# Transposed masks kept in DRAM: a graph-attention kernel on one Trainium2 core

## The chip, the cores and the metric

The kernel runs on one core of a Trainium2 chip. Time is device time in microseconds (us), median of several runs. The engines are TensorE (PE, matrix products; its weight loads are listed as PEld), VectorE (DVE), ScalarE (ACT), GpSimd (POOL) and SyncE (SP), which here does nothing but wait and issue DMAs. Each engine works off its own instructions in order.

## The reference, cut to what matters

```
x = layernorm(x + L0(x, adj))          # one attention stage over a 1024-node graph, 8 graphs, 256 features
mask = adj + eye > 0
for l in range(3):                     # the graph layers
    s_i, s_j = x @ attn_w[l, :256], x @ attn_w[l, 256:]
    scores = leaky_relu(s_i[:, None] + s_j[None, :] + attn_b[l], 0.2)
    attn = softmax(where(mask, scores, -inf))
    h = layernorm(x + attn @ x)
    x = layernorm(h + gelu(h @ W1[l] + b1[l]) @ W2[l] + b2[l])
out = layernorm(x_in + x)
```

`x` is (8, 1024, 256), `adj` (8, 1024, 1024), `W1` (3, 256, 1024). The mask is the same in all three layers.

## The kernel before, in words

A first stage (0 to about 575 us) computes `L0` and writes two things to DRAM: the rows `x` and an additive mask `mask`, bf16, 0 where there is an edge and -1e30 where not, by rows. Then come the graph layers. The unit is a chunk of 512 rows of one graph (BANK = 512); there are C = 16 chunks in a layer and K = 48 over three layers. In the loop over k every engine works on several chunks at once: TensorE transposes chunk k - 1's normalised rows (L1553), aggregates chunk k (L1575 to L1577), then runs chunk k - 1's feed-forward part, `up` (L43 to L45) and `down` (L1626 to L1628), over eight blocks f. One pass of that loop is called a step in what follows, "step k", counted from the transposes on L1553 at its head. Products are made of three passes over high and low parts; the low part is made by VectorE (`pT_lo` L1302, `g_lo` L1391, `h_lo` L1386), the high one by ScalarE.

The softmax numerator is needed with the neighbour j on the partitions, so the mask is needed transposed: `maskT`, [128, 8, 512] bf16, in two halves of four blocks. SP loads each half by a transposing DMA (`load_maskT`, L858), two chunks ahead. VectorE makes the unmasked scores `t` (L1295); GpSimd issues an accumulating DMA that adds `maskT` to `t` in SBUF, in four groups g (`add_masks`, L1100, semaphores `s_tm[g]`); ScalarE then takes the exponential twice (L1169, L1170). The untransposed mask is loaded too (`load_mask`, L851), a row block at a time into a ring of three, for the row maxima (`row_top`, L1281).

All of SP's DMAs stand in one order written out by hand. Per step it issues: `load_x` (even k, L843), `load_r` (odd k, L879), `load_raw` (L882, L884; raw weights of the next layer, steps 4 to 11 of a layer but the last), two row masks, at a new layer three pieces of the split weights (`load_split`, L907), the store of chunk k - 2's rows (L935), the first half of `maskT` for chunk k + 2, the store of `rline` (L872), `vline` (L863), `store_split` (L901), two more pieces, `load_v` (L868), `load_r`, two more masks, the second half of `maskT`, the last three pieces, and in the third layer only here the store of the output rows (L932). A wait in front of one of them holds all behind it.

At a layer's start TensorE computes a product of `b2` with all eight pieces of the new `W1` (`fold_b2`, L1604, 32 matmuls with two columns each) between the aggregation and the first `up`; it waits for all pieces. `raw_hi` (L1217) on ScalarE turns a raw piece into its high part, between the GELUs of blocks 1 and 2; `x_hi` (L1160) stands behind block 2. In the third layer ScalarE's `n2` (L1194) writes `xo`, and waits for the store of the chunk before.

Of the kernel before, what the change touches and what calls it, by code (L numbers as in the profile page):

```python
# [12 lines left out]
P = 128  # L13
F32 = mybir.dt.float32
F32R = mybir.dt.float32r
BF16 = mybir.dt.bfloat16
# [8 lines left out]
BANK = 512  # L25
# [602 lines left out]
def layer_buffers(nc, ctx, x, w1, rows, s_rows, uv):  # L628
# [3 lines left out]
    L = Layers()  # L632
# [7 lines left out]
    def sem(name):  # L640
        return ctx.enter_context(nc.semaphore(name))
# [135 lines left out]
    L.s_x_in = s_rows  # L777
    L.s_mask = [sem(f"mask_in{i}") for i in range(MASKS)]
    L.s_maskT = [sem(f"maskT_in{i}") for i in range(2)]
    return L  # L780


def graph_layers(nc, L, x, rows, out, mask, split, vline, rline, par):

    attn_w, attn_b, W1, b1, W2, b2, g1, be1, g2, be2 = par
    B, N, D, F, NT, KD, KF = shapes(x, W1)
# [42 lines left out]
    def tops_of(k):  # L829

        first = TC * k + NT + NT - 1
        return [r for r in range(first, first + TC) if r < NT * NB]

    with nc.Block() as block:
        @block.sync
        def _(sp):
# [16 lines left out]
            def load_maskT(k, half):  # L853
                if k > 0:
                    for g in range(2 * half, 2 * half + 2):
                        sp.wait_ge(L.s_tm[g], 16 * k)
                r = BANK * (k % C)
                sp.dma_start_transpose(L.maskT[:, HALF * half:HALF * (half + 1), :],  # L858
                                       mask_rows[r:r + BANK, BANK * half:BANK * (half + 1)]).then_inc(L.s_maskT[half], 16)

            def store_v(n):
                sp.wait_ge(L.s_vline, n - PB + 1)
# [87 lines left out]
            load_norm2(0)  # L950
            load_attention(1)
            for half in range(2):
                load_maskT(1, half)
            for r in range(NT, NT + NT - 1 + MASKS):
                load_mask(r)

            for k in range(K + 2):
                tops = tops_of(k)
                if k % 2 == 0 and k < K - 2:
                    load_x(k // 2 + 1)  # L960
                if 2 <= k and layer_of(k - 2) == LAYERS - 1:
                    load_x1(k - 2)
                if k % 2 == 1 and k + 2 < K:
                    load_r(k + 2)
                for f in split_at(k):
                    load_raw(layer_of(k) + 1, f)
                for r in tops[:2]:
                    load_mask(r + MASKS)
                arriving = layer_of(k) if k < K and new_layer(k) else 0
                if k == 0:  # L970
                    for f in range(2, KF):
                        first_weights(f)
                if arriving:
                    for f in range(3):
                        load_split(arriving, f)
                if k >= 2 and layer_of(k - 2) < LAYERS - 1:
                    store(k - 2)
                if k + 2 < K:
                    load_maskT(k + 2, 0)
                for n in r_made(k):  # L980
                    store_r(n)
                for n in v_made(k):
                    if n >= PB:
                        store_v(n)
                for f in split_at(k):
                    store_split(layer_of(k) + 1, f)
                if arriving:
                    for f in range(3, KF - 3):
                        load_split(arriving, f)
                for n in v_made(k):  # L990
                    if n >= PB:
                        load_v(n)
                for n in r_made(k):
                    load_r(2 * n)
                for r in tops[2:]:
                    load_mask(r + MASKS)
                if k + 2 < K:
                    load_maskT(k + 2, 1)
                if arriving:
                    for f in range(KF - 3, KF):  # L1000
                        load_split(arriving, f)
                if k >= 2 and layer_of(k - 2) == LAYERS - 1:
                    store(k - 2)
                if 2 <= k <= K and new_layer(k - 1):
                    load_norm2(layer_of(k - 1))
                    if layer_of(k - 1) + 1 < LAYERS:
                        load_attention(layer_of(k - 1) + 1)
# [658 lines left out]
def program(nc, x, adj, L0_W, L0_b, L0_attn, attn_w, attn_b, W1, b1, W2, b2, g1, beta1, g2, beta2, out):  # L1666
# [4 lines left out]
    layers = W1.shape[0]  # L1671
    rows = nc.dram_tensor("rows", (layers * C * TC, P, D), F32, kind="Internal").ap()
    mask = nc.dram_tensor("mask", (B * NT, P, N), BF16, kind="Internal").ap()
    split = nc.dram_tensor("split", (layers - 1, W1.shape[2] // P, P, 4, D), F32, kind="Internal").ap()
    vline = nc.dram_tensor("vline", (layers * B, N), F32, kind="Internal").ap()
    rline = nc.dram_tensor("rline", (layers * B, 2, N), F32, kind="Internal").ap()
# [3 lines left out]
    with ExitStack() as ctx:  # L1680
        x_rows = ctx.enter_context(nc.sbuf_tensor("x_rows", [P, 2, NT, D], F32))
        uv = ctx.enter_context(nc.sbuf_tensor("uv", [P, C, 2, TC], F32))
        s_rows = ctx.enter_context(nc.semaphore("x_in"))
        first_stage(nc, x, adj, L0_W, L0_b, L0_attn, attn_w[0], rows, mask, W1, x_rows, s_rows, uv)
        L = layer_buffers(nc, ctx, x, W1, x_rows, s_rows, uv)
        graph_layers(nc, L, x, chunks, out_chunks, mask, split, vline, rline, par)


# [22 lines left out]
```

## Time and profile before

| | |
|---|---|
| median of 3 runs | 2473.93 us (2473.46 to 2476.73) |
| the profiled execution's own time | 2465.25 us |
| its span | 2463.5 us |
| TensorE busy | 2317.7 us (94%) |
| VectorE, ScalarE, GpSimd busy | 2065.3, 1728.8, 1137.1 us |
| mean granted TensorE clock | 0.973 of 2.4 GHz |
| DMA | 399472 packets, 400.13 MB; 220408 packets under 512 B |

The profile is of one execution. Busy time says how long an engine had work, not how well it used it. TensorE's granted clock is either full (1.00, 2.4 GHz) or half (0.50, 1.2 GHz); the figure for a stretch is a mean. A DMA's time to landing counts from its issue to the last byte's semaphore.

### The profile page before, as it was taken

Reading aid. Unit: us, or ns where it says so; the run is one execution under the profiler, and the core shown is the slowest. Engines: PE = TensorE matmul, PEld = TensorE weight load, DVE = VectorE, ACT = ScalarE, POOL = GpSimd, SP = SyncE. Lnnn points to the kernel's source line nnn. Section 1 sums busy time; section 2 is a strip of 40 time slices with the busy share of each in tenths; the row PEclk is TensorE's granted clock in tenths of the full one; section 3 lists DMA queues with packets and bytes.
Section 4 is the critical chain, followed back from the end, with each engine's and each line's share of the span. In section 5 each row is a group of like instructions: output and inputs, shape, how many; then the busy total and the mean of one; then the engine's idle time right before and its main releaser. Section 6 shows DMA issues by size and latency. Waiting matters only on the chain.

```text
span 2463.5 us, 45033 instructions
## 1 busy us (share of the span) xinstructions
PE 2317.7 (94%) x16056; PEld 2136.5 (87%) x16056; DVE 2065.3 (84%) x4806; ACT 1728.8 (70%) x2780; POOL 1137.1 (46%) x1317
## 2 busy tenths in 40 slices
PE   7999999993499999999989999999999999999996
PEld 6999999993499999999979989999998888888996
DVE  5888888886678999998869989998997989889875
ACT  3444444442478888888858888888886788787784
POOL 3555555563234344554424434454453546545431
PEclk9999999996699999999989999999999999999998
DMA  4444444444657777775778677767776676685541
GB/s 144 141 141 140 139 145 149 140 129 97 177 145 192 174 189 197 195 178 161 187 174 193 154 189 198 184 180 189 189 174 171 173 198 160 166 206 148 135 112 43
DMA packets 399472, 400.13 MB, mean 162 GB/s; under 512 B 220408, under 2 KB 315152, under 8 KB 399248
## 3 DMA queue, kind: packets, MB, share of 16 engines
q1 hardware_dynamic: 371600, 296.58, 44.4%
q0 software_dynamic: 27648, 100.68, 17.8%
q8 instruction: 127, 2.08, 0.4%
q14 instruction: 97, 0.79, 0.1%
HBM read 187.19 MB, written 58.99 MB: 100 GB/s over the span
## 4 chain that ended last, share of the span: by engine, by line
PE 31%; DVE 18%; DMA 7%; ACT 6%; issue 6%; POOL 4%; SPq 4%; POOLq 0%; ACTq 0%; DVEq 0%
DVE t L1295 5%; PE A L1575 5%; PE A L1576 5%; PE A L1577 5%; DVE g_lo L1391 3%; SPq L858 3%; PE G L45 3%; PE G L43 3%; PE G L44 3%; PE Y L1626 2%; DMA t<-maskT 2%; PE Y L1628 2%; PE Y L1627 2%; DVE spare L1281 2%; DVE st L1321 1%
## 5 line engine op out<-in xcount | busy, mean ns | idle before, releaser
L1575 PE MATMUL A<-x_hi,pT_hi 128*128 128x258 f32 x1536 | 439.3, 286 | 31.5 <-DVE pT_lo L1302 25.2
L1626 PE MATMUL Y<-w,g_hi 128*128 128x256 f32 x1536 | 435.1, 283 | 10.6 <-DVE g_lo L1391 9.8
L1576 PE MATMUL A<-x_hi,pT_lo 128*128 128x258 f32 x1536 | 436.3, 284 | 0.0
L1577 PE MATMUL A<-x_lo,pT_hi 128*128 128x256 f32 x1536 | 433.7, 282 | 0.0
L1627 PE MATMUL Y<-w,g_hi 128*128 128x256 f32 x1536 | 426.8, 278 | 0.0
L1628 PE MATMUL Y<-w,g_lo 128*128 128x256 f32 x1536 | 426.4, 278 | 0.0
L1205 ACT ACTIVATE g<-G,b_less 128x512 f32<-128x512 f32 x384 | 263.6, 686 | 209.6 <-PE G L45 206.7
L1100 POOL DMA_DIRECT2D t<-maskT x192 | 173.8, 969 | 406.9 <-DVE t L1295 402.3
L1302 DVE TENSOR_TENSOR pT_lo<-t,pT_hi 128x512 fp32r<-128x512 f32 x384 | 256.1, 685 | 92.4 <-ACT t L1170 92.2
L1575 PEld LDWEIGHTS A<-x_hi,pT_hi 128*128 128x128 f32 x1536 | 292.5, 190 | 42.4 <-issue 24.2
L1391 DVE TENSOR_TENSOR g_lo<-g,g_hi 128x512 fp32r<-128x512 f32 x384 | 263.8, 687 | 69.4 <-ACT g_hi L1208 69.2
L1626 PEld LDWEIGHTS Y<-w,g_hi 128*128 128x128 f32 x1536 | 288.3, 188 | 33.3 <-DVE g_lo L1391 16.8
L43 PE MATMUL G<-h_hi,w 128*128 128x512 f32 x768 | 308.6, 402 | 5.8 <-DVE h_lo L1386 4.1
L45 PE MATMUL G<-h_lo,w 128*128 128x512 f32 x768 | 305.0, 397 | 0.0
L44 PE MATMUL G<-h_hi,w 128*128 128x512 f32 x768 | 303.6, 395 | 0.0
L1627 PEld LDWEIGHTS Y<-w,g_hi 128*128 128x128 f32 x1536 | 289.6, 189 | 10.6
L1577 PEld LDWEIGHTS A<-x_lo,pT_hi 128*128 128x128 f32 x1536 | 293.0, 191 | 0.0
L1576 PEld LDWEIGHTS A<-x_hi,pT_lo 128*128 128x128 f32 x1536 | 290.9, 189 | 0.0
L1628 PEld LDWEIGHTS Y<-w,g_lo 128*128 128x128 f32 x1536 | 288.7, 188 | 0.0
L1169 ACT ACTIVATE pT_hi<-t,v 128x512 fp32r<-128x512 f32 x384 | 273.1, 711 | 21.7 <-DMA t<-maskT 21.1
L1295 DVE SCALAR_TENSOR_TENSOR t<-rrow,v 128x512 f32<-128x512 f32 x384 | 280.8, 743 | 4.3 <-ACT rrow L1132 4.3
L1170 ACT ACTIVATE t<-t,v 128x512 f32<-128x512 f32 x384 | 272.3, 709 | 0.0
(190 smaller groups left out, 5921.6 us busy)
## 6 DMA issues: line engine op xcount, KB each, us to landing
t<-maskT POOLq DMA_DIRECT2D x192, 512.0 KB, 5.1
mask<-mask SPq DMA_DIRECT2D x192, 256.0 KB, 5.0
a_adj_t<-in_adj SPq DMA_DIRECT2D x64, 512.0 KB, 4.1
x_rows<-rows SPq DMA_DIRECT2D x24, 1024.0 KB, 6.3
rrow<-rline SPq DMA_DIRECT2D x92, 256.0 KB, 4.3
mask<-a_mask SPq DMA_DIRECT2D x64, 256.0 KB, 4.4
rows<-xo SPq DMA_DIRECT2D x32, 512.0 KB, 2.9
vrow<-vline SPq DMA_DIRECT2D x21, 512.0 KB, 4.6
```

Source lines behind the costliest of these rows:

```text
L43: pe.matmul(out, left_hi, right_hi, start=start, stop=False)
L44: pe.matmul(out, left_lo, right_hi, start=False, stop=False)
L45: return pe.matmul(out, left_hi, right_lo, start=False, stop=stop)
L1169: act.activation(L.pT[0][:, n % P_RING, :], L.t[:, j, :], ACT.Exp, bias=bias).then_inc(L.s_exp, 1)
L1295: dve.scalar_tensor_tensor(L.t[:, j, :], L.rrow[:, 0, k % 2, :], L.v8[:, k // 2 % VS, j:j + 1], L.rrow[:, 1, k % 2, :], ALU.add, ALU.max). ...
L1391: dve.tensor_tensor(L.g_lo[:, n % G_RING, :], L.g[:, n % 2, :], L.g_hi[:, n % G_RING, :].bitcast(F32), ALU.subtract).then_inc(L.s_g_lo, 1)
L1575: pe.matmul(L.A[:, t, 0:DE], hi, L.x_hi[:, par, j, :], start=(j == 0), stop=False)
L1576: pe.matmul(L.A[:, t, 0:DE], lo, L.x_hi[:, par, j, :], start=False, stop=False)
L1577: mm = pe.matmul(L.A[:, t, 0:D], hi, L.x_lo[:, par, j, :], start=False, stop=(j == NT - 1))
L1626: pe.matmul(L.Y[:, t, :], hi, w2_part(0, f), start=False, stop=False)
L1627: pe.matmul(L.Y[:, t, :], hi, w2_part(1, f), start=False, stop=False)
L1628: mm = pe.matmul(L.Y[:, t, :], lo, w2_part(0, f), start=False, stop=last and t % 2 == 1)
```

## The change

In the first layer each half of `maskT`, once loaded by the transposing DMA, is also stored as it stands in SBUF to a DRAM tensor `turned`. In the second and third layer `load_maskT` reads that half back with a plain DMA. The stores of chunk k + 1 stand at the head of step k (those of chunk 0 ahead of the loads for chunk 1), each behind a wait for the landing of its half. `load_maskT` waits, besides for `s_tm`, for the store of the chunk before.

```diff
+    L.s_maskT_out = [sem(f"maskT_out{i}") for i in range(2)]
...
                 if k > 0:
                     for g in range(2 * half, 2 * half + 2):
                         sp.wait_ge(L.s_tm[g], 16 * k)
+                    sp.wait_ge(L.s_maskT_out[half], 16 * min(k, C))
+                if k >= C:
+                    sp.dma_start(L.maskT[:, HALF * half:HALF * (half + 1), :], turned[k % C, half]).then_inc(L.s_maskT[half], 16)
+                    return
                 r = BANK * (k % C)
                 sp.dma_start_transpose(L.maskT[:, HALF * half:HALF * (half + 1), :],
                                        mask_rows[r:r + BANK, BANK * half:BANK * (half + 1)]).then_inc(L.s_maskT[half], 16)
+
+            def store_maskT(k, half):
+                sp.wait_ge(L.s_maskT[half], 16 * (k + 1))
+                sp.dma_start(turned[k, half], L.maskT[:, HALF * half:HALF * (half + 1), :]).then_inc(L.s_maskT_out[half], 16)
...
             load_attention(1)
             for half in range(2):
+                store_maskT(0, half)
+            for half in range(2):
                 load_maskT(1, half)
...
             for k in range(K + 2):
                 tops = tops_of(k)
+                if k + 1 < C:
+                    for half in range(2):
+                        store_maskT(k + 1, half)
                 if k % 2 == 0 and k < K - 2:
                     load_x(k // 2 + 1)
...
+    turned = nc.dram_tensor("turned", (C, 2, P, NT // 2, BANK), BF16, kind="Internal").ap()
```

## Rows read from the trace of the kernel before

**Rows 1.** Busy time in steps 9, 14, 17, 20, 21, 32, 33, 35 and 39.
```profile
core 0: us, PE busy (x) PEld busy (x) DVE busy (x) ACT busy (x) POOL busy (x), PEclk, DMA share, GB/s
...
964.60:1000.60 36.00, 35.85 (x259) 33.30 (x258) 32.97 (x77) 30.55 (x50) 16.06 (x16) 1.00 0.68 184
1108.40:1144.10 35.70, 35.70 (x260) 33.34 (x259) 32.38 (x76) 30.27 (x49) 15.46 (x16) 1.00 0.63 163
1251.00:1306.00 55.00, 45.78 (x291) 42.08 (x290) 33.09 (x78) 30.21 (x49) 14.47 (x16) 0.84 0.67 149
1378.10:1414.40 36.30, 35.83 (x259) 33.32 (x258) 32.98 (x77) 31.20 (x52) 18.59 (x26) 1.00 0.79 180
1414.40:1453.10 38.70, 36.77 (x259) 33.70 (x258) 33.21 (x77) 31.48 (x52) 10.28 (x16) 1.00 0.97 205
1812.20:1849.20 37.00, 36.26 (x259) 33.31 (x257) 32.47 (x76) 30.58 (x49) 18.96 (x26) 1.00 0.91 217
1849.20:1898.60 49.40, 44.76 (x291) 41.35 (x291) 32.71 (x78) 29.91 (x49) 15.46 (x16) 0.90 0.63 171
1935.60:1972.70 37.10, 35.91 (x260) 33.36 (x259) 33.45 (x73) 29.07 (x47) 19.97 (x18) 1.00 0.59 156
2084.80:2124.70 39.90, 36.44 (x259) 33.33 (x258) 33.64 (x73) 30.05 (x49) 19.97 (x18) 1.00 0.67 160
```

**Rows 2.** Waits, 690 to 2420 us: us in total, times, longest.
```profile
PE Y L1604 <- DMA w<-split: 12.8, 2, 8.6
...
ACT xo L1194 <- DMA out_rows<-xo: 11.7, 8, 3.7
```

**Rows 3.** SP's queue in step 17: start, duration of the issue, line.
```profile
1247.15 3.52 SPq L858 DMA_TRANSPOSE maskT<-mask  x1
...
1259.71 1.17 SPq L879 DMA_DIRECT2D rrow<-rline  x2
...
1261.92 4.68 SPq L858 DMA_TRANSPOSE maskT<-mask  x1
1266.64 1.53 SPq L907 DMA_DIRECT2D w<-split  x3
```

**Rows 4.** SP's queue in step 33.
```profile
1853.74 4.82 SPq L858 DMA_TRANSPOSE maskT<-mask  x1
1858.60 2.31 SPq L907 DMA_DIRECT2D w<-split  x3
```

**Rows 5.** Busy time behind the first fold, and in a stretch of step 16.
```profile
685.00:692.00 7.00, 7.00 (x24) 6.03 (x24) 3.27 (x9) 1.61 (x2) 0.00 (x0) 0.51 0.44 135
1248.00:1258.00 10.00, 10.00 (x85) 9.78 (x85) 8.13 (x21) 9.02 (x14) 0.16 (x1) 1.00 1.14 124
```

**Rows 6.** TensorE's timeline, the folds of the first and the third layer.
```profile
682.78 4.75 PE L1604 MATMUL Y<-b_parts,w 128*128 128x2 f32 x32
...
1866.22 6.99 PE L1604 MATMUL Y<-b_parts,w 128*128 128x2 f32 x32 [4.24 <-DMA w<-split]
```

**Rows 7.** Timelines and landings of L858 and L884, steps 9, 7 and 20.
```profile
969.04 4.94 SPq L858 DMA_TRANSPOSE maskT<-mask  x1
...
DMA to landing us min/median/max: 6.9/6.9/6.9
...
975.60 0.47 SPq L884 DMA_DIRECT2D x<-in_L_gnn_W  x1
...
DMA to landing us min/median/max: 4.4/4.4/4.4
...
981.24 0.63 ACT L1217 ACTIVATE x<-x 128x512 fp32r<-128x512 f32 x1
...
908.56 0.68 ACT L1208 ACTIVATE g_hi<-G,b_less 128x512 fp32r<-128x512 f32 x1
909.36 0.63 ACT L1217 ACTIVATE x<-x 128x512 fp32r<-128x512 f32 x1
...
1396.69 0.63 ACT L1217 ACTIVATE x<-x 128x512 fp32r<-128x512 f32 x1 [1.77 <-DMA x<-in_L_gnn_W]
```

More of the change, by code:

```diff
@@ L779, in layer_buffers, with graph_layers @@
     L.s_maskT = [sem(f"maskT_in{i}") for i in range(2)]
+    L.s_maskT_out = [sem(f"maskT_out{i}") for i in range(2)]
     return L
-def graph_layers(nc, L, x, rows, out, mask, split, vline, rline, par):
+def graph_layers(nc, L, x, rows, out, mask, turned, split, vline, rline, par):
     attn_w, attn_b, W1, b1, W2, b2, g1, be1, g2, be2 = par
@@ L1685, in program @@
         L = layer_buffers(nc, ctx, x, W1, x_rows, s_rows, uv)
-        graph_layers(nc, L, x, chunks, out_chunks, mask, split, vline, rline, par)
+        graph_layers(nc, L, x, chunks, out_chunks, mask, turned, split, vline, rline, par)
 _INS = ['x', 'adj', 'L0_gnn_W', 'L0_gnn_b', 'L0_gnn_attn', 'L1_gnn_attn_w', 'L1_gnn_attn_b', 'L1_gnn_W1', 'L1_gnn_b1',
```

## The prediction

> **What bounds the kernel now.** I cut the graph layers into steps, one for each pass of the loop over k, from one run of transposes on L1553 to the next, and read TensorE's busy time in each [rows 1]. In step 14 TensorE is busy for all 35.7 us: such a step can't get shorter by anything done to masks. Step 9, in which the weights of the next layer are split as well, takes 36.0 us with TensorE idle for 0.15. So the question is where TensorE idles, and the same view gives the places: step 17 (55.0 us, idle 9.2, mean granted clock 0.84), step 33 (49.4, idle 4.6, clock 0.90), step 21 (38.7), step 32 (37.0), step 39 (39.9), and step 35, one of the plain steps of the third layer, 37.1.
>
> The list of waits says what the idle time waits for [rows 2]. Two waits of the fold of b2 (L1604) for `w<-split` make 12.8 us, the longer 8.6, so the other 4.2: these are steps 17 and 33, where a new layer's weights arrive. ScalarE waits 8 times for the store of the output rows, 11.7 us in all, longest 3.7 (third layer). The third layer's plain steps are longer for another reason as well: step 35 takes 37.1 though ScalarE's waits for the store begin only after it, with VectorE at 33.45 us, more than in steps 9 and 14.
>
> Why are the weights late? The timeline of SP's queue in step 17 [rows 3]: SP is still occupied by the transposing DMA's issue for 3.52 us, and again for 4.68, and only then, at 1266.64, issues the last three pieces of `w`. In step 33 the same: 4.82 us of issue, then the three pieces [rows 4]. All DMAs that matter here stand in this one queue. A plain DMA of as much or more data takes SP about 0.5 us to issue (three in 1.53).
>
> There is a second effect. From 1248 to 1258 the DMA engines are counted as fully busy and move only 124 GB/s [rows 5]. In that stretch the 256-byte pieces of the transpose and the accumulating DMA of POOL (L1100) are under way together; the reload of `rrow` (L879), which waits for the small `rline` store ahead of it, goes out only at 1259.71 [rows 3].
>
> **What the change takes away.** 64 of the 96 transposes (layers two and three) become plain reads of 512 KB, 4 KB to a partition. For each, SP's issue falls from 3.5 to 4.8 us to about 0.5. Worked by places:
>
> Step 17. 3.0 us fall away on the first half's issue and 4.2 on the second's, 7.2 together; and from the end of the first half's issue (1250.67) to the reload at 1259.71 SP stood mostly for the slow stretch, which I take to go with the transposes: some 4 us more at the least, so that the last pieces go out about 11 us earlier than 1266.64. TensorE waited 8.6 us for them [rows 2]. So the wait is gone, not shortened. What is late next is the fold itself. Its price without a wait is seen in the first layer: 4.75 us against 6.99 [rows 6]. It begins there at the full clock (2.4 GHz), yet the clock falls during it, and from 685 to 692 the granted clock is 0.51, 1.2 GHz [rows 5]; of this 4.6 us lie behind the fold, at half speed, a loss of 2.3. A step that holds a fold and no wait is then 36.0 + 4.75 + 2.3 = 43.1 us. Gain in step 17: 55.0 - 43.1 = 11.9.
>
> Step 33. TensorE is free at 1866.22 - 4.24 = 1862.0 and the last piece landed at 1866.2 [rows 6]. Less 4.3 for the issue just ahead of it [rows 4] that is 1861.9, less again what the first half's issue gives: the wait is gone here too. Gain 49.4 - 43.1 = 6.3. If the clock's share were not to come back, the two steps would give 8.6 + 4.2 = 12.8 instead of 18.2.
>
> The Trainium skill ("TensorE: Matmul & The Clock Gate", the part on the HAM clock gate) says that idleness throttles TensorE and activity releases it; taken alone it would let the clock stay high once the wait is gone. The trace does not agree for the fold: rows 5 show 0.51 behind a fold that had no wait before it, though its matmuls of two columns kept the engine occupied. I go by the row; by the page alone the two steps would give some 4 us more.
>
> Step 21 has the same slow stretch and ScalarE's late masks and weights; without it 36.0: gain 2.7. Step 32: 37.0 to 35.7, gain 1.3.
>
> Third layer. SP stores the output rows only behind the second mask half. With both halves short the store goes out some 6 us earlier, the longest wait for it was 3.7, so all eight go. About 0.9 us of each was absorbed: step 39 waited 3.7 and was 39.9 against 37.1, so 2.8 counted. The other seven, 8.0 us together, count 8.0 - 6.3 = 1.7. Gain 4.5, not more, since step 35 shows 37.1 without such a wait.
>
> Sum of gains: 11.9 + 6.3 + 2.7 + 1.3 + 4.5 = 26.7 us.
>
> **What it adds.** 32 stores of 512 KB in the first layer, about 0.5 us of issue each. TensorE doesn't see the 16 us, SP has idle time in each step. The added wait of `load_maskT` for the store is free: the store goes out at the start of a step, the load in its middle or end, and even the transposing DMA of the same size lands within 6.9 us [rows 7]. In layers two and three that wait is for a count reached long before.
>
> What costs is where the stores stand. `store_maskT(k + 1, 1)` waits at the head of a step for a transpose that SP has only just issued. In step 9 the issue ran from 969.04 for 4.94 us and the DMA landed after 6.9, so SP stands for 2.0 us [rows 7], and 0.5 for the second store (the first is issued in the waiting time). Behind it in the queue are `load_x`, `load_r`, `load_raw` and two mask loads; all go out 2.5 us later. Their data then also stand behind 512 KB that were just put on the engines: up to 1.5 us more. Bounds for the delay: 2.0 (wait only) to 5.0 (wait, issue, both stores' data in front); I take 3.0, near the wait plus issue. `load_r` and the masks have many microseconds to spare. `load_raw` (steps 4 to 11) has not: in step 9 its second part landed at 975.60 + 4.4 = 980.0, used at 981.24, 1.2 to spare; in step 7 L1217 starts at 909.36, 0.12 after the GELU before it ended (908.56 + 0.68): ScalarE was waiting already, nothing to spare [rows 7]. ScalarE waits for it in order, with the GELUs behind it, then VectorE's `g_lo`, then TensorE. How much lateness is absorbed shows step 20: ScalarE waited 1.77 us there and the step took 36.3, 0.3 over step 9 [rows 1, 7]; so 1.5 is free. With a delay of 3.0: a step like 7 costs 1.5, a step like 9 costs 0.3. Three steps like 7 and five like 9: 6.0 us. At 2.0 it is 1.5, at 5.0 3 x 3.5 + 5 x 2.3 = 22. `load_x` (every even step) comes ahead of `load_raw` and its use is later in the step; I cost it at nothing beyond that. In the start-up (before step 1) two stores also stand before `load_x(1)`; VectorE needs the result a few us later than it comes: nothing, at most 1.5.
>
> Net: 26.7 - 6.0 = 20.7 us off the profiled execution's 2465.25. That lies 8.7 us under the median of the runs shown; taken as an offset, 2473.93 - 20.7 = 2453.
>
> **The rivals.** A (the forecast, 0.60): as above, 2453. Without any loss in the first layer it would be 2447; should the unprofiled runs owe their 8.7 us more to further slow stretches, 2438.
>
> B (0.22), the gain is half of this: the slow stretch of DMA stays, made by the accumulate with any load beside it. Then the `rline` reload is held up as before, and of 11.9 us in step 17 remain the 4.2 of the second half's issue; steps 21 and 32 give nothing. 4.2 + 6.3 + 4.5 - 6.0 = 9, time 2465. For it: the stretch is the DMA engines' state, and plain reads of the same bytes will be in flight with L1100 too. Against: the packets that crawl are 256 bytes, and there will be none. With the larger first-layer cost (22) B ends at +7; between them lie results within 0.2% (5 us).
>
> C (0.10), slower: the wait at the head of SP's queue. It decides from a delay of about 6.0 us: 3 x 4.5 + 5 x 3.3 = 30 against 26.7. This takes stores that land late enough to hold the loads behind them by 3 us more than I take, in each of the eight steps, with `x_rows` late as well. For it: the engines are loaded there (0.68 of their time in step 9). Time 2477 to 2485.
>
> D (0.08), the change does nothing on the path: the issue time of SP doesn't matter. The Trainium skill ("DMA: Bandwidth & Descriptors", Issuing engines are not separate DMA queues) says the time to initiate a DMA is usually small beside the DMA. By that rule the weights and the output store would land no earlier. Worked out from the rows, steps 17 and 33 and the third layer then stay as they are, and 2.7 + 1.3 - 6.0 is a loss of 2 us: 2476. Rows 3 and 4 speak against it: 4.68 and 4.82 us of issue immediately ahead of the late pieces.
>
> **Numbers.** About 0.2% (5 us) is what this measurement can tell from no change. Faster by more: all of A, most of B, 0.81; within: 0.11; slower: 0.08. Range 2438 (A with the offset regained) to 2468 (B with a somewhat larger loss).
>
> **What would show it.** In the trace after: the two waits L1604 for `w<-split` gone, steps 17 and 33 at about 43 us; SP's plain issue about 0.5; no ScalarE wait for `out_rows`, third-layer steps still 37.1; steps 4 to 11 at 36 to 37.5 with ScalarE idle before L1217. Wrong if those steps grow by over 3 us each, or if `w<-split` still lands last.

## The result and the profile after

The changed kernel takes 2449.74 us (median of 4 runs, 2446.57 to 2455.83); the kernel before took 2474.28 (4 runs, 2473.46 to 2476.73). The ratio is 0.9902, 95% interval 0.9882 to 0.9923: 24.5 us faster, where 20.7 were forecast. A later comparison (kernel 5) gave 2445.72 against 2480.77, ratio 0.9861 (0.9832 to 0.9890). The profiled execution after took 2449.08 us, 16.2 less than the profiled one of before (2465.25). So the profile shows two thirds of the medians' difference; where the rest lies is a question for the experiments.

The steps after, in the same view as [rows 1]: steps 6, 9, 17, 21, 32, 33 and 39.

```profile
core 0: us, PE busy (x) PEld busy (x) DVE busy (x) ACT busy (x) POOL busy (x), PEclk, DMA share, GB/s
...
860.60:898.20 37.60, 36.15 (x260) 33.53 (x259) 33.16 (x77) 31.88 (x53) 13.16 (x26) 1.00 0.93 248
971.30:1007.40 36.10, 35.93 (x260) 33.38 (x259) 32.96 (x77) 29.64 (x48) 11.46 (x16) 1.00 0.79 207
...
1259.10:1302.60 43.50, 41.55 (x291) 38.20 (x290) 32.73 (x78) 30.34 (x49) 15.48 (x16) 0.96 0.60 194
1410.20:1446.20 36.00, 35.87 (x259) 33.34 (x258) 32.95 (x77) 30.37 (x49) 16.07 (x16) 1.00 0.61 178
1805.20:1840.90 35.70, 35.68 (x260) 33.33 (x259) 32.46 (x76) 30.27 (x50) 18.02 (x26) 1.00 0.73 215
1840.90:1887.30 46.40, 44.26 (x291) 40.97 (x290) 32.89 (x78) 30.11 (x49) 15.47 (x16) 0.89 0.57 187
2072.10:2109.20 37.10, 35.90 (x259) 33.35 (x258) 33.62 (x73) 30.15 (x49) 19.99 (x18) 1.00 0.59 172
```

Step 17 went from 55.0 to 43.5 us, step 21 from 38.7 to 36.0, step 32 from 37.0 to 35.7 and step 39 from 39.9 to 37.1. Step 33 came down by 3.0 only, to 46.4, and its granted clock is still 0.89. Step 6 grew from 36.1 to 37.6, as did steps 4, 8 and 11 to between 36.9 and 37.4, while step 9 stayed at 36.1 (36.0 before). The waits that answer to [rows 2], with ScalarE's for the raw weights:

```profile
ACT x L1231 <- DMA x<-in_L_gnn_W: 11.0, 4, 3.1
...
PE Y L1618 <- DMA w<-split: 3.6, 2, 2.1
...
ACT xo L1208 <- DMA out_rows<-xo: 1.1, 2, 0.8
```

The fold waits 3.6 us in all for the split weights, in place of 12.8, and ScalarE 1.1 in place of 11.7 for the output store. New are four waits of ScalarE for the raw weights in the first layer, 11.0 us. SP's queue in step 17 and at the end of its part for step 33, beside [rows 3] and [rows 4]. L860 is the plain read, L916 the split weights, L888 the reload of `rrow`:

```profile
1256.21 0.95 SPq L916 DMA_DIRECT2D w<-split  x2
1259.31 0.85 SPq L888 DMA_DIRECT2D rrow<-rline  x2
...
1261.87 0.33 SPq L860 DMA_DIRECT2D maskT<-turned  x1
1262.24 1.49 SPq L916 DMA_DIRECT2D w<-split  x3
...
1844.71 0.37 SPq L860 DMA_DIRECT2D maskT<-turned  x1
1845.12 1.38 SPq L916 DMA_DIRECT2D w<-split  x3
```

The last three pieces now leave at 1262.24, 3.1 us into the step (before, 15.6 us into it); the reload of `rrow` leaves 3.1 us after the pieces ahead of it, where it took 8.4. The issue of a turned mask half in layers two and three, L860 after:

```profile
L860 SPq DMA_DIRECT2D maskT<-turned x63: 319/327/369, 1188.5 to 2333.0; - x63
...
DMA to landing us min/median/max: 3.4/5.1/7.4
```

and L858 before, over the same layers (ns, minimum/median/maximum, then the landing):

```profile
L858 SPq DMA_TRANSPOSE maskT<-mask x63: 1519/4198/5420, 1184.4 to 2349.6; - x63
...
DMA to landing us min/median/max: 4.0/6.8/12.4
```

So the issue went from a median of 4.2 us to 0.33, and the longest landing from 12.4 us to 7.4. The busy stretch of [rows 5] looks like this after; the last two numbers are the DMA engines' busy share and GB/s:

```profile
1248.00:1258.00 10.00, 10.00 (x71) 9.26 (x70) 10.00 (x27) 7.72 (x13) 5.50 (x5) 1.00 0.95 261
1258.00:1268.00 10.00, 10.00 (x85) 9.80 (x85) 8.11 (x20) 10.00 (x17) 1.52 (x2) 1.00 1.03 348
```

As busy as before, but at 261 and 348 GB/s in place of 124. The first layer shows what was paid. SP's queue in step 6 (L863 transposes, L868 stores, L844 is `load_x`, L891 and L893 are `load_raw`) and ScalarE's reading of the raw weights:

```profile
865.18 5.79 SPq L863 DMA_TRANSPOSE maskT<-mask  x1
871.02 2.37 SPq L868 DMA_DIRECT2D turned<-maskT  x2
873.48 0.38 SPq L844 DMA_DIRECT2D x_rows<-rows  x1
873.91 0.98 SPq L891 DMA_DIRECT2D x<-in_L_gnn_W  x1
874.93 0.69 SPq L893 DMA_DIRECT2D x<-in_L_gnn_W  x1
...
880.48 0.63 ACT L1231 ACTIVATE x<-x 128x512 fp32r<-128x512 f32 x1 [3.09 <-DMA x<-in_L_gnn_W]
```

SP has the first store out at 871.02; the second goes out 2.1 us later, when the transpose lands (7.9 us after its issue), and `load_raw` leaves behind both. Its data land at 880.5, and ScalarE has stood idle for 3.09 us.

### The profile page after: what moved, and what is told of

The parts are those of the page before. It is cut to its first block, busy times and chain, and to the rows that moved or that the text cites. A ratio compares the mean times of both kernels' runs of the same rounds, so it can differ in the third digit from the quotient of the medians.

```text
span 2447.2 us, 45065 instructions
## 1 busy us (share of the span) xinstructions
PE 2316.0 (95%) x16056; PEld 2136.8 (87%) x16056; DVE 2064.6 (84%) x4806; ACT 1729.0 (71%) x2780; POOL 1105.9 (45%) x1317
## 3 DMA queue, kind: packets, MB, share of 16 engines
q0 software_dynamic: 27648, 100.68, 17.1%
## 4 chain that ended last, share of the span: by engine, by line
PE 36%; DVE 19%; DMA 6%; ACT 5%; issue 4%; POOL 4%; SPq 2%; POOLq 0%; ACTq 0%; DVEq 0%
PE A L1589 6%; PE A L1590 6%; PE A L1591 6%; DVE t L1309 6%; DVE g_lo L1405 3%; PE G L45 3%; PE G L43 3%; PE G L44 3%; PE Y L1640 3%; PE Y L1641 3%; PE Y L1642 3%; DVE spare L1295 2%; DMA t<-maskT 1%; DMA x<-in_L_gnn_W 1%; DVE st L1335 1%
## 5 line engine op out<-in xcount | busy, mean ns | idle before, releaser
L1589 PE MATMUL A<-x_hi,pT_hi 128*128 128x258 f32 x1536 | 440.2, 287 | 30.2 <-DVE pT_lo L1316 24.3
```

Source lines behind the costliest of these rows:

```text
L1589: pe.matmul(L.A[:, t, 0:DE], hi, L.x_hi[:, par, j, :], start=(j == 0), stop=False)
```

## The experiments

Each kernel was timed beside the kernel before on the same chip; in the table "before" is its median there. "Spread" is from the lowest to the highest run. The two columns of steps are from the one profiled execution of each: length, the fold's wait for the split weights, and the time at the half clock (1.2 GHz) in that step, added up from stretches of 1 us.

| kernel | median, us | before | ratio (95%) | spread | step 17: us / wait / half clock | step 33 |
|---|---|---|---|---|---|---|
| before, profiled first | | 2474.28 | | 3 | 55.0 / 8.6 / 17.1 | 49.4 / 4.2 / 10.2 |
| changed | 2449.74 | 2474.28 | 0.9902 (0.9882-0.9923) | 9 | 43.6 / 1.4 / 3.4 | 46.4 / 2.1 / 10.2 |
| 1 wait only | 2480.85 | 2477.26 | 1.0015 (0.9998-1.0032) | 17 | 56.4 / 9.8 / 20.5 | 51.2 / 5.7 / 13.7 |
| 2 store only | 2480.68 | 2477.26 | 1.0013 (0.9997-1.0030) | 14 | 52.0 / 6.9 / 13.7 | 49.4 / 4.1 / 13.7 |
| 3 plain, no store | 2448.45 | 2477.26 | 0.9879 (0.9862-0.9896) | 4 | 45.5 / 1.3 / 10.2 | 47.1 / 2.0 / 10.2 |
| 4 order only | 2473.62 | 2477.26 | 0.9981 (0.9966-0.9996) | 17 | 42.0 / 0 / 3.4 | 43.9 / 1.3 / 6.8 |
| 5 changed, again | 2445.72 | 2480.77 | 0.9861 (0.9832-0.9890) | 6 | 41.5 / 0 / 3.4 | 45.9 / 1.3 / 10.2 |
| 6 late store | 2443.57 | 2480.77 | 0.9853 (0.9821-0.9885) | 8 | 46.1 / 1.4 / 10.2 | 43.2 / 1.2 / 3.4 |
| 7 late store and split | 2440.96 | 2480.77 | 0.9837 (0.9808-0.9867) | 9 | 44.1 / 0 / 6.8 | 43.5 / 0 / 6.8 |
| 8 small accumulate | 2440.91 | 2480.77 | 0.9838 (0.9808-0.9867) | 10 | 47.7 / 3.4 / 10.2 | 47.4 / 2.3 / 10.2 |
| 9 plain at two chunks | 2459.71 | 2477.47 | 0.9934 (0.9908-0.9959) | 14 | 42.4 / 0.4 / 3.4 | 42.5 / 0.9 / 3.4 |
| 10 plain elsewhere | 2459.05 | 2477.47 | 0.9931 (0.9904-0.9958) | 20 | 57.9 / 9.8 / 17.1 | 49.0 / 3.8 / 13.7 |
| 11 plain everywhere, late split | 2436.00 | 2477.47 | 0.9838 (0.9808-0.9867) | 8 | 43.9 / 0 / 6.8 | 42.5 / 0 / 3.4 |
| 12 before, again | 2475.53 | 2479.95 | 0.9979 (0.9940-1.0018) | 27 | 55.4 / 9.2 / 17.1 | 48.1 / 3.7 / 10.2 |

### 1 and 2. The wait alone, and the stores with it

The kernel before with only the wait at the head of the steps:

```diff
                 tops = tops_of(k)
+                if k + 1 < C:
+                    for half in range(2):
+                        sp.wait_ge(L.s_maskT[half], 16 * (k + 2))
```

> The kernel before, with SP waiting at the head of steps 0 to 14 for both halves of the next chunk's mask, and no store. Theory Q (the cost in the first layer is SP's queue held up by the wait, and what is behind it comes late): of the 4.4 us that the first layer lost in the profile after, the wait of some 2.0 us alone gives the smaller part, 1 to 2.5 us in steps 4 to 11, and nothing in any other step. Rival S (the loss is made by the stores' own data on the DMA engines): 0 us. Rival N (the loss is chance of one execution): steps 4 to 11 unchanged, and it will not come again in the next run either.

The second kernel has all of the change but the plain reads: stores and waits as in the diff, and transposes in all three layers.

> The changed kernel with the plain reads taken out: waits and stores in the first layer, transposing DMAs in all three. Theory Q: steps 4 to 11 lose the same as in the profile after, 4 to 5 us, in the same steps (4, 6, 8, 11), the rest is the kernel before: 3 to 6 us slower. Under S the same total, but then the run with the wait alone shows nothing. Under N no loss. Also told apart: the 3.7 us by which the changed kernel was late before step 1. If the added tensor or the stores ahead of step 0 made them, they come again here; if it was chance of the first stage, whose code is the same, they don't.

With the wait alone two of the steps 4 to 11 grew, step 5 to 36.3 and step 11 to 36.7 us, about 1 us in all, though ScalarE waited 0.2 to 2.2 us for the raw weights in six of them. With the stores as well, five steps grew to between 36.4 and 37.6, 4.7 us in all. The changed kernel lost 4.4 us in steps 4 to 11. So most of the first layer's cost comes with the stores that go out ahead of `load_raw`, their bytes and the second one's issue. That the wait alone costs anything is not shown: kernels 3 and 4 below, whose first layer is that of the kernel before, lost 1.1 us in the same two steps 5 and 11. Over the whole kernel both are within 0.2% of before: without the plain reads there is no gain.

### 3. Plain reads without stores

The adjacency is symmetric, so rows of the mask are also its columns. In layers two and three the turned half is read from the row mask (pieces of 1 KB), and nothing is stored:

```diff
+                if k >= C:
+                    n, c = k % C // NCH, k % NCH
+                    sp.dma_start(L.maskT[:, HALF * half:HALF * (half + 1), :],
+                                 mask[NT * n + HALF * half:NT * n + HALF * (half + 1), :, BANK * c:BANK * (c + 1)]
+                                 .rearrange("t p i -> p t i")).then_inc(L.s_maskT[half], 16)
+                    return
```

> The kernel before, with plain reads in the second and third layer and no store at all: the adjacency of these inputs is symmetric, so the transposed half is read directly from the row mask, in pieces of 1 KB instead of 4 KB. Theory: all of the gain from step 17 on and none of the loss: in the profile after that gain was 24.3 us, so 22 to 26 us faster than before; steps 4 to 11 as before. Rival L (the gain hangs on the 4 KB pieces of the stored copy): with 1 KB pieces the steps 17 and 33 keep more of their wait, gain under 15 us. A gain much over 26 us would say that the first layer loses more in the unprofiled executions than in the profile.

This gave 28.8 us, more than the 22 to 26 expected, and five runs lay within 3.5 us. The expectation would have put such a surplus down to a larger loss in the first layer outside the profile; kernel 6, which has no such loss, is only 2.2 us faster than the changed kernel beside it, so the surplus is not explained by that. Steps 21, 32 and 39 are at 36.0, 35.6 and 37.2 us as in the changed kernel: the gain is that of the missing transposes, not of a stored copy. Steps 17 and 33 kept waits of 1.3 and 2.0 us here too.

### 4. The order alone

The kernel before, with the last three split pieces issued ahead of the second mask half; every transpose stays:

```diff
-                if k + 2 < K:
-                    load_maskT(k + 2, 1)
                 if arriving:
                     for f in range(KF - 3, KF):
                         load_split(arriving, f)
+                if k + 2 < K:
+                    load_maskT(k + 2, 1)
```

> The kernel before, transposes and all, with only the last three pieces of the new layer's weights put ahead of the second mask half in SP's order (steps 16 and 32). Theory Q (issue time of the transpose just ahead of the pieces): the pieces go out 4.7 us earlier; in step 33 the wait of 4.2 us is gone and with it part of the slow clock, 4 to 6 us; in step 17 4.7 of 8.6 us go: together 8 to 11 us faster, all in steps 17 and 33. Rival D (the time of issue doesn't matter, the data's way does): both steps keep their waits, under 2 us. Steps 21, 32 and the third layer unchanged under both.

The two steps 17 and 33, and SP's queue from the loads in step 16 on:

```profile
1254.40:1296.40 42.00, 41.41 (x291) 38.11 (x290) 32.75 (x78) 30.38 (x49) 15.48 (x16) 0.96 0.69 185
1844.90:1888.80 43.90, 42.62 (x291) 39.35 (x290) 32.79 (x78) 29.60 (x49) 15.48 (x16) 0.92 0.69 194
...
1247.66 4.28 SPq L858 DMA_TRANSPOSE maskT<-mask  x1
...
1256.37 0.80 SPq L879 DMA_DIRECT2D rrow<-rline  x2
...
1258.16 2.39 SPq L907 DMA_DIRECT2D w<-split  x3
1260.65 5.98 SPq L858 DMA_TRANSPOSE maskT<-mask  x1
```

The pieces left at 1258.16, ahead of a transpose of 5.98 us of issue. Steps 17 and 33 fell by 13.0 and 5.5 us with all transposes in place. In step 33 the order is what changed: the reload of `rrow` stands 2.7 us into the step as before, the pieces left 4.5 us into it and not 9.4, and the wait fell from 4.2 to 1.3 us. In step 17 two things came together. The pieces left 3.7 us into the step and not 15.6, but the reload ahead of them already left at 2.0 in place of 8.7, since here the first half's transpose was issued 6.7 us ahead of the step (at 1247.66) and not 3.9, and landed after 8.5 us and not 12.4. So 6.7 of those 11.9 us are not the order's.

The expectation was 8 to 11 us, all in these two steps; the median gained 3.6 (interval 1.0 to 8.4), a miss. The profiled execution is the lowest of twelve, and in it steps 22, 27 and 45 were 40.5, 40.4 and 39.0 us, which had been 36.1, 36.1 and 35.7. What steps 17 and 33 were in the other eleven runs is not known. Fixing the order leaves the other thing that transposes do.

### 5 to 7. The changed kernel, its stores moved, its split pieces moved

Kernel 5 is the changed one. Its step 17 had no wait and took 41.5 us, 2.1 less than in the first profile; so much does one kernel vary there. Kernel 6 moves the stores in the step:

```diff
-                if k + 1 < C:
-                    for half in range(2):
-                        store_maskT(k + 1, half)
...
                 for f in split_at(k):
                     load_raw(layer_of(k) + 1, f)
+                if k + 1 < C:
+                    for half in range(2):
+                        store_maskT(k + 1, half)
```

Kernel 7 is kernel 6 with all five remaining split pieces together:

```diff
-                    for f in range(3, KF - 3):
+                    for f in range(3, KF):
                         load_split(arriving, f)
...
-                if arriving:
-                    for f in range(KF - 3, KF):
-                        load_split(arriving, f)
```

> The changed kernel once more, as the base for the two edits of it that run on the same chip. Every theory expects about 0.990 of the kernel before, with its runs close together (about 2446 to 2456 us, against some 2467 to 2486 for the kernel before), step 17 at about 43.5 us and step 33 at about 46.4, and waits of ScalarE for raw_hi of 2 to 3 us in three or four of the steps 4 to 11.

> The changed kernel with the two stores of a step moved from the head of SyncE's step to behind the load of raw, ahead of the first two mask rows. If what the first layer pays is the wait of the stores at the head of SyncE's queue, which holds the load of raw back (my theory), the waits for raw_hi of 2.4 to 3.1 us in steps 4, 6, 8 and 11 go, these steps come back from 36.9-37.6 to about 36.1 us, and the kernel is 3 to 6 us faster than the changed one. Rival: the first layer pays for the stores' bytes beside its other transfers, wherever they are issued: then these steps stay at about 37 us and the time is that of the changed kernel within 1 us. Second rival: a store issued later makes the next transpose, which waits for it, late enough for the matmuls behind it; then waits for the turned masks would appear in the first layer and the steps would be longer than 37 us. Steps 17 and 33 are as in the changed kernel by all three (43.5 and 46.4 us).

> The kernel of the run before, with the last three split weight pieces of steps 17 and 33 issued right behind the third and fourth, ahead of the loads of the second mask half. If the rest of the wait for the split weights (1.44 us in step 17, 2.13 us in step 33) is still the order in SyncE's queue, the wait goes and step 17 falls to about 42 us and step 33 to 43-44, 3 to 5 us in all. Rival: the transfers are then limited by the DMA engines and not by their issue, since the pieces took 9.6 us from issue to landing in step 33: the three pieces land hardly earlier, step 33 stays at 46 us or above, and less than 2 us is won in all, or the mask rows that now come later cost as much.

SP's queue in step 6 of kernel 6:

```profile
866.70 5.12 SPq L863 DMA_TRANSPOSE maskT<-mask  x1
871.91 0.53 SPq L844 DMA_DIRECT2D x_rows<-rows  x1
872.49 0.57 SPq L891 DMA_DIRECT2D x<-in_L_gnn_W  x1
873.12 0.46 SPq L893 DMA_DIRECT2D x<-in_L_gnn_W  x1
873.62 1.06 SPq L868 DMA_DIRECT2D turned<-maskT  x2
```

The raw weights leave right behind the transpose, and the stores after them. All of steps 5 to 11 are at 36.0 to 36.1 us in kernels 6 and 7, step 4 at 36.3: the 4.4 us are gone, with as many bytes stored as before. The rival that bytes cost wherever they stand falls.

In the profile, that is: the median of kernel 6 lies only 2.2 us under kernel 5's, less than the 3 to 6 expected, and the intervals overlap. The two profiles differ elsewhere by as much: kernel 6 lost 4.7 us in step 17, where its clock stood at half for 10.2 us and not 3.4, and won 2.8 in step 33, where it was the reverse. Steps 17 and 33 of kernel 7, and its fold:

```profile
1254.80:1298.80 44.00, 43.15 (x290) 39.76 (x289) 32.76 (x78) 30.37 (x49) 15.47 (x16) 0.92 0.60 194
1837.80:1881.30 43.50, 42.91 (x292) 39.63 (x291) 32.81 (x78) 30.42 (x49) 15.46 (x16) 0.92 0.58 188
...
1267.93 5.43 PE L1615 MATMUL Y<-b_parts,w 128*128 128x2 f32 x32 [0.46 <-ACT xo L1205]
```

The wait for the split weights is gone in both; the fold waits 0.46 us for ScalarE. Yet step 17 takes 44.0 us and not 42, since the clock stayed at half for 6.8 us of it. The later split was expected to give 3 to 5 us over kernel 6 and gave 2.6, with runs that overlap; step 33, 43.5 us where 43 to 44 was expected, was 43.2 in kernel 6 already. Kernel 7 is 4.8 us under kernel 5, and their runs hardly touch (2434.88 to 2443.52 and 2443.50 to 2449.82); the two edits together were expected to give 6 to 11.

### 8. The accumulating transfer cut down

The kernel before, but POOL's accumulate moves 16 of 512 columns. It leaves out nearly all of the addition of the turned mask.

```diff
-  pool.dma_start(L.t[:, 2 * g:2 * g + 2, :], L.maskT[:, 2 * g:2 * g + 2, :], accum_op=ALU.add)
+  pool.dma_start(L.t[:, 2 * g:2 * g + 2, 0:16], L.maskT[:, 2 * g:2 * g + 2, 0:16], accum_op=ALU.add)
```

> The kernel before, with the accumulating transfer of POOL cut to 16 of its 512 columns; it leaves out nearly all of the addition of the turned mask to the scores. The transposes stay, all 48. Theory: a transpose becomes slow (10 to 13 us to its landing) when it is in flight together with the accumulating transfer, and it is this that makes single steps long at changing places and the times of one kernel spread over 15 to 20 us. Then here no transpose lands after more than 9 us, no step outside 17, 33 is over 38 us, and the runs lie within about 5 us of each other; steps 17 and 33 keep most of their waits, which come from the issue time (step 17 above 50 us if its stretch of 11 us is issue time, about 46 if half of it was the collision). Rival: the transposes are slow by themselves or against the other plain loads: late landings and long steps appear as often as before (a dozen landings over 8.5 us) and the spread stays near 15 us.

The first half's transpose for chunk 18, which took 12.4 us to land in the kernel before; a stretch with the second half's; and all transposes of layers two and three:

```profile
1243.55 2.10 SPq L858 DMA_TRANSPOSE maskT<-mask  x1
...
1248.70:1258.70 10.00, 10.00 (x86) 10.00 (x86) 7.88 (x18) 10.00 (x17) 3.73 (x7) 1.00 1.08 257
...
L858 SPq DMA_TRANSPOSE maskT<-mask x63: 1302/2223/6844, 1176.9 to 2326.4; - x63
...
DMA to landing us min/median/max: 3.9/4.6/10.5
```

The transpose that had crawled now lands after 4.6 us, though an accumulate was issued 0.22 us behind it. The median landing is 4.6 us instead of 6.8, and even the median issue on SP fell to 2.2 us from 4.2. One of 63 landed after more than 9 us (10.5, where none was expected), and of steps 2 to 47 only 17 and 33 are over 37.4. Step 17 is 47.7 us: of the 11.4 us that it lost between the kernels before and after, 7.3 go with the accumulate alone; the rest stays, with a wait of 3.4 us behind SP's issues. The runs spread over 10 us, not the 5 expected, but no longer 25 like the kernel before beside it. The median is 39.9 us under the kernel before, but this kernel computes something else.

A transpose with no accumulate in flight doesn't crawl, in this kernel (257 GB/s from 1248.70 to 1258.70) or in the kernel before: from 1262.0 to 1268.5, around the second half's transpose, the engines moved 228 GB/s at a busy share of 1.03, and 124 in [rows 5]. Its pieces are 256 bytes in both stretches (the 64 transposes that the change takes out are 131584 of the packets under 512 bytes, 2056 for each 512 KB). The Trainium skill ("DMA: Bandwidth & Descriptors", Why small descriptors are slow) gives 27% of overhead for a 256-byte descriptor; the trace shows that size alone does not make the slow stretch, 228 and 124 GB/s at the same size.

Nor does being in flight together suffice. The thirteen profiles other than this kernel's hold 768 transposes. Of these 360 were in flight with an accumulate, and most landed as soon as the other 408: the medians are 6.6 and 6.9 us. But all 23 that took more than 10 us are among the 360. The moment of issue tells them apart: 51 transposes were issued on SP within 0.3 us of an accumulate's issue on POOL, and 23 of these landed after 10.2 to 14.9 us (median of the 51: 9.7); of the other 717 none took over 9.9. In [rows 5] the transpose was issued at 1247.15 and the accumulate at 1247.31, and both took 12 us. So the crawl belongs to the pair, and it comes only when the two are issued almost at once; as the engines' phase shifts from step to step, that happens at changing places. No run here sets that distance on purpose, and 28 of the 51 landed within 10 us all the same.

### 9 and 10. Plain reads at two chunks, and at all others

Both are kernel 3 with another condition in its first line: `if k in (18, 34):` (the two chunks whose masks load beside the split weights, four transposes of 96), and `if k >= C and k not in (18, 34):`.

> The kernel before with plain loads of the turned mask (read from the row mask, which is symmetric) in place of four of its 48 transposes only: those of the two chunks whose loads stand beside the split weights in steps 17 and 33. Theory: there the transposes cost by their issue and by the collision with POOL's accumulating transfer, so step 17 falls to about 44-46 us and step 33 to about 46-47, some 13 us in the profile; but the other 28 transposes of layers two and three still collide now and then, so the runs stay spread over 15 us and the median is 12 to 16 us under the kernel before, short of the 28.8 us that plain loads everywhere in both layers gave. Rival: all that plain loads give lies in those two steps; then this kernel is 25 us or more faster and its spread is that of the plain kernels, a few us.

> The complement of the run before it: plain loads in layers two and three except for the two chunks whose loads stand beside the split weights, which keep their four transposes. Theory: steps 17 and 33 stay at about 50 to 55 and 48 to 50 us, while steps 21, 32 and 39 fall to 36.0, 35.6 and 37.1 us and no step elsewhere is a stretch too long; 8 to 10 us by the profile and 12 to 16 us by the median, with runs within 10 us of each other. Rival: nothing but steps 17 and 33 matters, and this kernel is within 3 us of the kernel before.

Steps 17 and 33 of kernel 9:

```profile
1254.20:1296.50 42.30, 41.54 (x291) 38.15 (x290) 32.71 (x78) 30.30 (x49) 15.47 (x16) 0.96 0.62 175
1836.90:1879.40 42.50, 41.47 (x291) 38.22 (x291) 32.86 (x78) 30.36 (x49) 11.45 (x16) 0.96 0.68 201
```

and of kernel 10:

```profile
1256.30:1314.20 57.90, 45.82 (x292) 42.12 (x291) 33.11 (x78) 30.17 (x49) 10.45 (x16) 0.85 0.72 160
1852.60:1901.60 49.00, 45.17 (x292) 42.00 (x291) 32.81 (x78) 30.20 (x49) 15.47 (x16) 0.86 0.61 174
```

Four plain reads give 17.8 us, the other 60 give 18.4; 12 to 16 had been expected of each, and both came out above. The gain has two halves, and the first profile had shown little of the second. They are not parts of one sum: together they are 36.2 us, where kernel 3, with all 64, gave 28.8 on another chip, and each interval is 13 us wide. So the shares are rough. Kernel 9 took step 33 to 42.5 us, which is the size that the prediction gave it. Of kernel 10 the spread was misjudged: 20 us, where under 10 was expected. Its profiled execution has nothing slow in layers two and three outside steps 17 and 33, and a landing of 14.9 us for the transpose in step 17; so by the spreads (20 us here, 14 in kernel 9) these two steps may vary as much as all the others together; one profile of each cannot show it.

### 11. No transposes, late split

> No transpose and no store at all: the turned mask is read by plain loads from the symmetric row mask in all three layers, and the last three split pieces stand ahead of the second mask half. By the issue theory the first layer gains nothing (its loads of raw have 3 to 6 us of slack in the kernel before), step 17 is at 41.5 to 42.5 us without a wait for the split weights and step 33 at 43.2 to 44 us, and the whole is at 2435 to 2442 us, about that of the late-store-and-split kernel (2440.96) less the 1 us or so which its first layer still loses. Rival: pieces of 1 KB are dearer than the stored copy's of 4 KB when the DMA engines are saturated, and in step 33 the time stays at 46 us or above, 2443 us or more in all; this rival is the weaker since 1 KB pieces lost no more than 0.7 us in step 33 and nothing elsewhere in the earlier run.

Kernel 3 with plain reads in the first layer as well, and the order of kernel 7. 2436.00 us, the lowest median of all; as a ratio it equals kernel 7 (0.9838 and 0.9837). The first layer's steps stayed at 36.0 to 36.3: nothing was to be had there, though the raw weights now came 3.5 us or more before their use. (The expectation gave them 3 to 6 us of slack in the kernel before; there it was 0 to 3.4.)

### 12. The kernel before, again

> The kernel before, profiled a second time. The execution profiled first (2465.25 us) lies at or under the lowest of 55 other runs of the same kernel, so its steps should understate what the transposes cost. Theory: the second one is nearer to 2475-2480, and what it has more lies in layers two and three, in single steps at other places than 21, 32 and 39 and in step 17 or 33 (transposes landing after 10 us or more beside them), while the first layer's steps 4 to 11 are again 36.0 to 36.3. Rival: the difference is in the first stage or in the granted clock of all steps; then layers two and three are step for step as in the first profile.

Of this profile (2473.07 us): the DMA engines over 10 us, step 25, the transposing DMA ahead of it with its landing, and the reload of `rrow` behind it:

```profile
1562.00:1572.00 10.00, 10.00 (x85) 9.82 (x85) 6.98 (x20) 6.87 (x12) 1.72 (x4) 1.00 1.27 84
1563.30:1604.90 41.60, 37.46 (x258) 33.58 (x257) 33.08 (x77) 31.78 (x53) 9.80 (x16) 1.00 0.93 180
...
1559.51 3.29 SPq L858 DMA_TRANSPOSE maskT<-mask  x1
...
1573.90 0.80 SPq L879 DMA_DIRECT2D rrow<-rline  x2
...
DMA to landing us min/median/max: 14.2/14.2/14.2
```

Steps 4 to 16 are as in the first profile to 0.1 us. What is new stands where the first profile had nothing: step 25 at 41.6 us (36.05 there) and step 45 at 40.0 (35.7), while step 32, long there, is 35.65. A transpose issued ahead of step 25, 0.02 us before an accumulate, landed after 14.2 us, the engines moved 84 GB/s, and the reload left 10 us after the last DMA ahead of it. Eight runs reached from 2455.86 to 2483.23, so the first profile was a low one but not the lowest possible.

## Why the prediction was right

**Step 17** (11.9 us): 11.4 measured. The wait was forecast as gone and fell from 8.6 to 1.4, and the clock recovered after 3.4 us at half, where 4.6 was assumed. Two errors of opposite sign. (In kernel 5 the same step had no wait and took 41.5.)

**Step 33** (6.3 us): 3.0 measured, the term that was mis-sized. "The wait is gone here too" was wrong: it fell from 4.2 to 2.1 us. The last three pieces left 4.2 to 5.2 us into the step, but they took 6.9 to 9.6 us to land; behind a transpose (before) they had landed 5.0 to 5.7 us after their issue. The masks, the reload and the weights now go out within a few microseconds and share the engines, which is the likely reason and was not tested by itself. And the half clock lasted 10.2 us, as before. The relation between the columns of the table tells how much each counts: less the wait and half of the time at the half clock, steps 17 and 33 are 39.2 to 40.8 us in the changed kernel and in kernels 5, 6, 7, 9 and 11. That is step 9's 36.0 and a fold of 3.6: the fold takes 3.63 us wholly at the full clock (first layer of the changed kernel) and 6.99 wholly at half [rows 6], so the forecast's 4.75 held a part of the clock's loss already. The forecast had 6.8 us at half in each of the two steps, 3.4 of loss (1.1 of it inside the 4.75); by the relation the 10.2 us in step 33 cost 5.1.

What sets this time can be read from the traces. In each of the 14 profiles the clock fell once in step 17 and once in step 33, and rose again 2.8 to 5.9 us behind the end of the fold. How long it was down followed the moment of the fall: 3.4 us where it fell 3.3 us or more after the fold's start, 6.8 where it fell 1.7 to 3.0 us after it, 10.2 from 0.2 us ahead of it to 1.4 after it, and 13.7 to 20.5 where it fell 0.8 us or more ahead, during the wait (in step 17 of the kernel before at 1268.7, with the fold from 1273.45 on). A wait is not needed, since in kernel 7 it fell 1.7 us into a fold that had waited 0.46 us for ScalarE. Nor does a short wait decide: 3.4 us behind 1.4 us in step 17 of the changed kernel, 10.2 behind 1.4 in that of kernel 6. What sets the moment of the fall stays open.

**Steps 21 and 32** (2.7 and 1.3): 2.7 and 1.4. **Third layer** (4.5): 4.3; the two waits for the store that are left cost nothing, and the plain steps stayed at 37.1. Steps 18 and 34, which the forecast left out, gave 0.9 and 0.6.

**First layer** (cost 6.0): 4.4 in steps 4 to 11. SP stood 2.1 us for the transpose in step 6 (forecast 2.0). The second raw piece landed 2.2 us earlier to 6.1 us later in its step than before, 2.3 later on average over the eight steps, where a delay of 3.0 was taken. The "up to 1.5 us more" behind the stores' data is in no run by itself, and the 6.9 us within which a transpose was said to land held for that one: in the kernel before some took up to 12.4. That step 9 would pay little and step 7 more was wrong in its places (steps 4, 6, 8 and 11 paid): the phase of SP in a step shifts from step to step. Kernels 2 and 6 show that it was the position of the stores.

**Start-up** (0, at most 1.5): in the first profile the start of step 1 is 3.0 us later, and its end 3.7: in that profile the second mis-sized term. Across the other kernels that end lies at 709 to 717 us where nothing is stored and at 714 to 720 where it is (kernels 2 and 5 to 7), so some 3 us may be the stores'; with ranges that overlap this stays open.

**The rivals.** B said that the slow stretch is made by the accumulate with any load beside it. Its condition is refuted: 261 and 348 GB/s after, with the accumulate in place beside plain loads. C was right in the place and wrong in the price: it needed a delay of 6 us in each of the eight steps, and only step 8 had that (6.1 us). D, that the issue time of SP doesn't matter, by the Trainium skill's rule ("DMA: Bandwidth & Descriptors", Issuing engines are not separate DMA queues) that it is usually small: kernel 4 took 5.5 us from step 33 by letting the weights' pieces go out before a transpose's issue, though its median gained no more than 3.6. The trace does not agree with the rule for transposes here: a median issue of 4.2 us stands beside a median landing of 6.8.

**The median against the profile.** The forecast took the 8.7 us between the profiled execution and its median as an offset that stays. They were at least in part what the change removes: long steps at changing places, from transposes that meet the accumulate. In the profile the terms add up to 11.4 + 3.0 + 2.7 + 1.4 + 4.3 + 0.9 + 0.6 = 24.3 us of gain and 4.4 + 3.7 of cost, 16.2 net, 4.5 short of the 20.7 forecast. By the medians it was 24.5, 3.8 above. The mechanism was right; that the number came so near is in part luck, since two misses went opposite ways. The prediction named the further slow stretches for its lower end, but gave them no share in the forecast.

## What to carry to other kernels

Count the issue time of a DMA on its queue, by kind: a transpose that stood ahead of the weights cost step 33 5.5 us in the profile by its place alone. Where two DMAs of different kinds crawl together, look at the distance of their issues and not only at whether they overlap. Where a profiled execution lies well below the median, ask which random loss it happened to miss, since a change may remove just that; one more profile of the kernel before would have shown steps 25 and 45. And do not read an edit's worth from one profile: kernel 4's showed 18.5 us in two steps, its median 3.6. A store that must wait for a landing belongs behind the loads that have no slack: moving it behind them took its cost of 4.4 us out of the profile.

## What was not expected of the hardware

- A transposing DMA and an accumulating one issued within 0.3 us of each other can crawl: 23 of 51 such transposes landed after 10.2 to 14.9 us, and none of 717 others after more than 9.9. In two such stretches the DMA engines, fully busy, moved 124 and 84 GB/s. Transposes without an accumulate beside them moved 228 and 257 GB/s, accumulates beside plain loads 261 and 348, equally busy.
- The issue of the same transpose on SP takes 1.3 to 7.6 us, and its median falls from 4.2 to 2.2 us when the accumulate beside it is small: it is not a fixed cost of issuing.
- The granted clock falls to half (1.2 GHz) in or right behind a fold of 32 matmuls of 2 columns though TensorE hardly idles (0.46 us ahead of it in kernel 7), and stays there for 3.4 to 10.2 us in kernels whose steps hold the same work, the longer the earlier in the fold it fell. Not every fold does it: behind the first layer's in kernel 3 the clock did not fall.
